# A fourth stream for the attention head, six shared q/k places and an in-place bias in a three-block decoder kernel

## The chip, the cores and the metric

One Trainium2 chip, one core. The metric is device time in microseconds (us) for one execution over the whole batch; it is the median of several runs. Engines: TensorE (PE, with its weight loads PEld), VectorE (DVE), ScalarE (ACT), GpSimd (POOL), SyncE (SP, which here only issues DMAs).

## The reference, cut to what matters

32 sequences of 256 tokens by 512 features pass one post-norm decoder layer of three blocks, each followed by a residual and a layernorm:

```
x = layernorm(x + attention(x, Wqkv, Wout))        # 16 heads of 32, rotary, causal, window 256
x = layernorm(x + mlstm(q=x, k=ctx, v=ctx))        # 4 heads of 128, gates, log-decay, RMS norm
x = layernorm(x + routed_attention(x))             # 4 of 16 heads of 64 picked per sequence,
                                                   # q/k/v with bias, softmax, @ Wo + bo
```

The heads of the third block are picked by a softmax over the token mean of `x @ Wr + br`, so their weights are fetched from HBM by an index that is known only on the chip.

## The kernel before, in words

**Stages and streams.** For each sequence b there are three stages: `stage_a` (first block), `stage_b` (second) and `stage_c` (third). Every engine has a generator for each stage, which does one small step (a group of transposes, one projection, one copy) and yields. Three streams, a, b and c, run over all 32 sequences; `in_turns` merges them by lists, one per engine: a letter says which stream's next step the engine issues. `FILL` starts the pipeline, `ORDER` is repeated `STEADY = NB - 4` = 28 times, one turn for each sequence, and `DRAIN` ends it. In a turn the engines work on stage a of sequence b+1, stage b of b and stage c of b-1. Nothing else sets the order: each engine works its list strictly in order, and semaphores hold it where something isn't ready.

**PSUM.** Four banks `ps_s` hold attention scores, four others are a ring `ps_g`; `BANKS` says which bank of the ring each step uses, and `plan()` derives what must have emptied it (`freed`).

**Stage a.** x is transposed (2 steps), split by ACT (L1033) and DVE (L1288) into a high and a low part `x_t`, and projected with three products per operand pair (L672, `mm3`). For each of four quads of heads (`rotary(u)`) DVE shuffles (L1298) and multiplies by the cosine (L1301), POOL multiplies by the sine (L1655), DVE adds (L1305). `values(t)` gives v. Then per quad: scores, maxes (DVE L1312), exponentials (ACT L1025), transposes of the probabilities (`turn`, copied by ACT L1076 and DVE L1341), product (`att`), scaling (L1358), split (L1103, L1362), and the output projection, the residual (DVE L1368), statistics, `rstd` (POOL L1643, L1645) and x1 (DVE L1381, two instructions). The attended values are written over x_t (`att_t = x_t`), so x of the next sequence can't be split before the output projection of this one is done.

**Stage b.** Transposes of ctx and x1 (copied by ACT L1121), the products for the gates (copied by ACT L1127), gate (DVE L1403), |f| (L1406), exp and ln on ACT, log f (L1410), its running sum on PE (`cum`), a scan, decays, the products c and h, the RMS norm and layernorm, x2 (DVE L1485).

**Stage c.** Transposes of x2, router (`logit`, DVE L1500 to L1524; its index is ready after L1514), the fetch of the picked weights by SP (L648, into `p_all`, `pt_all` and `y_out`), their split (ACT L1188, DVE L1534), q, k, v, scores, softmax, transposes (`fturn`), product (`fatt`, split by ACT L1025 and DVE L1575), output projection (`wo`). POOL adds the bias bo to x2 beforehand (L1707, two instructions), into a tensor of its own, `x2_bo`; DVE adds the projection (L1610); after the layernorm ACT writes `y_out` and stores it (L1256).

**Order around the change, before.** In a steady turn TensorE's list reads, from the end of the output projection of b (b+1, b-1 written as +1, -1):

```
out0 out1 | x2T0-1 xT0+1 ctxT0 xT1+1 ctxT1 x1T0 x2T1-1 x1T1 | qk0+1 gate_t logit-1 gate v0+1 cum SC0+1 a_row
v1+1 m_col decay0 qk1+1 decay1 c0 c1 c2 c3 g-1 SC1+1 h00 h01 h10 h11 ... qk2+1 qk3+1 fturn0-1 ... fturn1-1 att0+1 ...
turn4..7 fturn2-1 att1 fturn3-1 SC3 fatt1-1 turn8..11 wo0-1 att2 wo1-1 turn12..15 att3 out0 out1
```

(`xT`, `x1T`, `x2T`, `ctxT` are transposes, `SC` scores, `v0` is two half steps.)

Of the kernel before, what the change touches and what calls it, by code (L numbers as in the profile page):

```python
# [12 lines left out]
P = 128  # L13
# [48 lines left out]
    "sync": (
        "aaaaaaaaaaaaaaaaaaaaaaaaaaaaaaaaaaaaabaaaaaaaaaaaaaaaaaaaaabaaaaaaaaaaabaaaaaaaaaaaaaaaaaaaaaaaaaaaaaaaaaabaaa"
        "aaaaaaaaaaaaaaaaabaaaaaaaaabaaabaaaaaaaabaabaabaaaabaaaaaaaabaaaabbbaaaabaabaabbbaaaabaabaabbbababaabbaabbaaaa"
        "abaaabaaaacbabbabbbaabbabbbabbbaabbbbaaaaaaaabaabaaaaaabababaaaaaaaaacabaaaaaaaccaabcaaacaaaaabaaaaccaaaccaacb"
        "aaccacaabcaaabaaaaacacaacacacabcacaaabaacaabaccacbcbacaaacababcabacacaaaaaaabbaccccbaaabaaabaabaaccababacacaaa"
        "bacaccbcabbabaaabbbaccbacbcccaabccabaabaaaacaacbccaaaaacacbacbbbcbbbaabc"
# [19 lines left out]
    "gpsimd": (
        "abacbaaababccabaacaabcbbbbaccbabbcccacaabbabbabbabababbcbabcbbbaccbacbabacabccaaabbccbbbbacbccccbaaabbcabbaabc"
        "baaabacccacaaaaaacacccaaacaaaaaaaacaaacaacaacaaacaccaccaccacaaaacaaabaaaaccaacaaaaacaacaaacaaabaaaaaaaacaacaac"
        "aaacabca"  # L90
    ),
    "sync": (
        "acaacaaaccbccbcaabaabbccabaaccbaaabccbbbbbabcacacccccaaaaabababaacbaacacaaabacaaaaaaabcbaaaaacaacabbaacaaaaaaa"
        "aaaabacbabaabbcaacabacbaacaaccabcaccbaabaaaccaacaaacbbbaaaabbaaacaccaccbcacaabaacaababaccaaaccbcbcbbacaccabbaa"
        "aaacbbca"
# [5 lines left out]
        "babcabbcababcbacbababcbbaaabcbbabaababaacacaababbbbbabcbbbcbbcaabcbbacabbbcccaabbbcababbcacccccaaacaccaacaccab"  # L101
        "caaaaccaccacacaaccacacacaacaaaccaacacaaccaccaacbaaaaabcabacaaacaaaaaaacacaaaaaccaaacaaaaaabaaacaaaaabcaaababbc"
        "abaacbabaaabbbbcbbcbccbbbbcbbbbbbbbbbbcbbbccbbbbcbbbcbcccbacbcbccbcccbcccccccccccaccccccbcccccccbcccccbccccccc"
        "cccccccccccccccbccccccccccccccccccccbccccbccccbcccccccccccbcaccccccccc"
    ),
    "scalar": (
        "cbcaababacbabbabbbacacabbcabcbbcabbbababbaaaabcaababcabaaabbcccbbcbacbccbcabbcbabbbbcbacbcbabbabccaccaaacccbaa"
        "cccaaccacaabaaacbacaacacacaaccaaccacaacaacacccacaaaaacacaacaacaacaaaaacaaaaaaacbaaaaaaaaacaaaacaaaabaaaabacaab"
        "abaccbbbcbbabcbaaabbbbbbcbcbbcbcbbbabbabbcbbbbcbbbbccbcbcbccbcccbbbccbcbbccccccccccbccccccccccccccccccccccccbc"
        "ccccaccbcccccccbcccccccccccccccccccbcccccccccccccbcccccccccccccccccccc"  # L110
    ),
    "vector": (
        "babbabcaabbbccabbcaaabbabacabcbcbcbbbcaaabaaaaabbbbaabbbaabbabbbccbcbbbabcbbabbabacabbacccabcaabccacbcccbbcaca"
        "cacaaaacaabcccccacccacaacacaacaccaaccacacaaacaacaacaacaaaaccbbaacaaabcaaabaaaacaaaaaacacacacaaabacababaaaaabab"
        "baaaaabaaacaaccaaaabaaccbcbcbbcbbbbbbcbcbbbcbbbbbbbcbbbcbccbccbcccccccccbbbcccccbcbbbccccccbcccccccccbcccccbcc"
        "ccbcccccbccccccccccccccccccccccccccccccccccccccccccccccccccccccccccccc"
    ),
    "gpsimd": (
        "babcbaabacaccbcbabbbcbabcacbabbbbbbbabbabcaaacbaaaaabaaabcacabbbbbabcabacbacabcbbaaacaacbabcbcabccccabbababbab"
        "bccccacacaaccaaaaccaaacacabaacaaaaaccaaaaaaacaaaacaacaacacabaaaaaaaaacbacccacaaacaaccaaccacbcacaccaacaaaaabaac"  # L120
        "ccabcabbabbaacbacbabbcbabcbbbabbbccbcbccbcbbbbccacccbbbbccbccbcbcbcbbbbccccccbccbbccbbccbcbcccccbccbccccccccbc"
        "ccbcccccccccccccccccccccccccccccccccbccccccccccccccccccccccccccccccccc"
    ),
    "sync": (
        "bcaacabbbaabcaaabaaccaababaaaaaacaaaaaabacbcacaacacbbaaaacbcaabacccbacacaacacabaabaaacacaaacbaaaaccaacaacaccca"
        "bbbaaabbcaaccacbbabccbcaaacbacbccaabaccaccbbcabaacbaaaaaabaabacacbbacbccacaaaaabcabbccccabbccbbacacaacbaacabbc"
        "abbbaacabaaaaacacbaccbccbcbccbcccbcccbcccccbbbbbcccbbbbcbccbcbccbbcccccbcccbbbcccbcbbccccccccbcccccbccbbcbcccb"
        "ccbbbcccbcccbbccccccccccccbccccccccccbcccccccbccccccbccccbcccbccccbccc"
    ),
}  # L130

BANKS = {
# [4 lines left out]
}  # L137

RING = 4
STEADY = NB - 4  # L140
# [53 lines left out]
def build(nc, x, ctx, wqkv, wout, igk, igb, fgk, fgb, rms, wq, bq, wk, bk, wv, bv, wr, br, wo, bo, out):  # L194
# [3 lines left out]

    def halves(name, shape):
        return [sb(f"{name}_{part}", shape, F32R) for part in ("hi", "lo")]  # L200

    def part(pair, *at):
        return [h[at] for h in pair]

# [1599 lines left out]
```

## Time and profile before

| | before |
|---|---|
| median of 3 runs | 2482.59 us (2482.21 to 2490.61) |
| the profiled execution | 2486.7 us, span 2485.0 us |
| busy: PE, DVE, ACT, POOL | 2239.6, 1880.7, 1427.3, 723.9 us |
| mean granted TensorE clock | 0.975 |

The span runs from the first to the last instruction; busy time of an engine is the union of its instructions. A matmul's end is modelled, so a busy PE is not PE at its peak, and short stalls are partly hidden by the tail of the matmul before them. The numbers of L... lines are those of the kernel's file.

### The profile page before, as it was taken

How to read it: one execution, taken by the hardware profiler on the slowest of the kernel's cores; microseconds unless marked ns; L12 is line 12 of the kernel's file. 1: busy time of each engine (PE TensorE's matmuls, PEld its weight loads, DVE VectorE, ACT ScalarE, POOL GpSimd, SP SyncE). 2: the span in 40 equal slices, each digit the busy share in tenths (PEclk: the TensorE clock that was granted, in tenths of full speed). 3: DMA queues.
4: the chain of work that ended last, by engine and by line, in shares of the span. 5: the costliest groups of instructions: out<-in, count | busy, mean ns of one | idle time of the engine just before them, and what ended most of it. 6: DMA issues, size and time to landing. Idle time of an engine off the chain costs nothing.

```text
span 2485.0 us, 55639 instructions
## 1 busy us (share of the span) xinstructions
PE 2239.6 (90%) x20672; PEld 1870.6 (75%) x20672; DVE 1880.7 (76%) x4586; ACT 1427.3 (57%) x4586; POOL 723.9 (29%) x1069
## 2 busy tenths in 40 slices
PE   5888999999999999999999999999999999999864
PEld 4677777877777887778787777878777788877753
DVE  4567788777788877788877787887778788777753
ACT  4445665556566556566655656665665665565632
POOL 2112233222223322323332322332322233222321
PEclk9989999999999999999999999999999999999976
DMA  4010111121011112011121101122211112210111
GB/s 118 18 44 22 49 35 52 52 52 42 29 44 44 52 52 52 27 44 39 48 52 52 44 27 49 38 52 52 52 40 30 44 44 52 52 52 10 43 26 43
DMA packets 267472, 109.94 MB, mean 44 GB/s; under 512 B 215234, under 2 KB 248258, under 8 KB 267202
## 3 DMA queue, kind: packets, MB, share of 16 engines
q1 hardware_dynamic: 258498, 89.61, 14.6%
q10 hardware_dynamic: 8704, 16.78, 1.8%
q8 instruction: 164, 2.69, 0.5%
q14 instruction: 106, 0.87, 0.1%
HBM read 89.57 MB, written 16.78 MB: 43 GB/s over the span
## 4 chain that ended last, share of the span: by engine, by line
PE 44%; DVE 24%; ACT 14%; POOL 5%; issue 5%; SPq 4%; DMA 3%; POOLq 0%; DVEq 0%
PE ps_g L672 32%; PE ps_g L680 10%; ACT p_a L1025 4%; SPq L648 3%; PE ps_s L672 2%; DVE neg_max L1312 2%; DMA y_out<-in_L_ffn_Wv 2%; DVE x_tok L1368 2%; POOL h_ssq L1688 2%; POOL qk_rot L1655 2%; DVE qk L1305 2%; DVE qk_rot L1298 1%; ACT p_all L1025 1%; DVE ctx_t L1473 1%; POOL p_all L1743 1%
## 5 line engine op out<-in xcount | busy, mean ns | idle before, releaser
L1025 ACT ACTIVATE p_a<-ps_s,neg_max 128x128 f32<-128x128 f32 (+1 forms) x1024 | 416.9, 442 | 59.8 <-DVE neg_max L1312 59.7
L672 PE MATMUL ps_g<-x_t_hi,wqkv_hi 128*128 128x256 f32 x1024 | 295.9, 289 | 13.4 <-DVE x_t_lo L1288 13.1
L672 PE MATMUL ps_g<-x_t_lo,wqkv_hi 128*128 128x256 f32 x1024 | 288.6, 282 | 0.0
L672 PE MATMUL ps_g<-x_t_hi,wqkv_lo 128*128 128x256 f32 x1024 | 288.2, 281 | 0.0
L1312 DVE TENSOR_REDUCE neg_max<-ps_s 128x2 f32<-128x256 f32 (+1 forms) x512 | 256.0, 541 | 4.4 <-PE ps_s L672 3.6
L1743 POOL TENSOR_SCALAR p_all<-p_all,f_rec,g_bc 128x256 f32<-128x256 f32 x256 | 144.9, 576 | 359.2 <-DVE f_rec L1561 359.2
L680 PE MATMUL ps_g<-const,p_a 128*128 128x128 f32 x1536 | 225.8, 282 | 15.5 <-ACT p_t L1076 9.2
L1655 POOL TENSOR_TENSOR qk_rot<-qk_rot,const 128x512 f32<-128x512 f32 x128 | 163.8, 1280 | 246.8 <-DVE qk_rot L1298 246.4
L1025 ACT ACTIVATION_READ_ACCUMULATOR p_a<-ps_s,neg_max 128x1 f32 x1024 | 233.8, 228 | 0.0
L680 PEld LDWEIGHTS ps_g<-const,p_a 128*128 128x128 f32 x1536 | 171.7, 143 | 58.8 <-ACT p_t L1076 29.1
L672 PEld LDWEIGHTS ps_g<-x_t_hi,wqkv_hi 128*128 128x128 f32 x1024 | 196.7, 192 | 15.2 <-issue 13.5
L672 PEld LDWEIGHTS ps_g<-x_t_lo,wqkv_hi 128*128 128x128 f32 x1024 | 197.3, 193 | 0.1
L672 PEld LDWEIGHTS ps_g<-x_t_hi,wqkv_lo 128*128 128x128 f32 x1024 | 196.2, 192 | 0.0
L1025 ACT ACTIVATE p_all<-ps_g,f_bias,g_bc 128x256 f32<-128x256 f32 x256 | 142.3, 560 | 68.4 <-DVE f_bias L1556 62.3
L672 PE MATMUL ps_g<-x_t_hi,w_sel_hi 128*128 128x256 f32 x512 | 151.7, 296 | 8.7 <-DVE w_sel_lo L1534 7.5
L1358 DVE TENSOR_TENSOR att_s<-ps_g,r_bc 128x256 f32<-128x256 f32 x128 | 54.3, 424 | 134.2 <-ACT r_bc L1098 131.9
L672 PE MATMUL ps_g<-x_t_hi,w_sel_lo 128*128 128x256 f32 x512 | 143.8, 281 | 0.0
L672 PE MATMUL ps_g<-x_t_lo,w_sel_hi 128*128 128x256 f32 x512 | 143.7, 281 | 0.0
L1195 ACT COPY v_f<-ps_g 128x512 f32<-128x512 f32 x32 | 18.8, 586 | 209.1 <-PE ps_g L672 209.1
L1341 DVE COPY p_t<-ps_g 128x384 f32<-128x384 f32 x256 | 136.0, 541 | 3.7 <-PE ps_g L680 3.6
L1076 ACT COPY p_t<-ps_g 128x384 f32<-128x384 f32 x256 | 119.3, 480 | 23.0 <-PE ps_g L680 20.7
L672 PE MATMUL ps_s<-qk 32*128 32x256 f32 (+1 forms) x2048 | 121.2, 351 | 7.6 <-DVE qk L1305 3.5
(203 smaller groups left out, 6377.0 us busy)
## 6 DMA issues: line engine op xcount, KB each, us to landing
x_tok<-in_x SPq DMA_DIRECT2D x32, 512.0 KB, 3.6
ctx<-in_ctx SPq DMA_DIRECT2D x64, 256.0 KB, 3.4
p_all<-in_L_ffn_Wq SPq DMA_DIRECT2D x128, 128.0 KB, 2.6
pt_all<-in_L_ffn_Wk SPq DMA_DIRECT2D x128, 128.0 KB, 3.0
y_out<-in_L_ffn_Wv SPq DMA_DIRECT2D x128, 128.0 KB, 3.1
out<-y_out ACTq DMA_DIRECT2D x32, 512.0 KB, 2.8
x<-in_L_attn_Wqkv SPq DMA_DIRECT2D x2, 512.0 KB, 9.6
p_all<-in_L_attn_Wqkv SPq DMA_DIRECT2D x1, 512.0 KB, 6.5
```

Source lines behind the costliest of these rows:

```text
L648: engine.dma_start(w_raw[j][:, :, k, :], col((wq, wk, wv)[j])[:, :, bass.ds(picks[k], DF)]).then_inc(w_loaded[j].sem, 16)
L672: return nc.tensor.matmul(o, l, r, start=first, stop=last)
L680: return nc.tensor.transpose(o, i, ident)
L1025: return nc.scalar.activation(o, i, f, **kw)
L1076: nc.scalar.copy(p_t[:, 2 * p % 4, :], bank[("turn", 2 * p), b][:, 0:CAUSAL]).then_inc(act_emptied.sem)
L1305: v.tensor_tensor(qk[:, 2 * u:2 * u + 2, :], qk[:, 2 * u:2 * u + 2, :], qk_rot, ALU.add).then_inc(roped.sem)
L1312: m = v.tensor_reduce(neg_max[i][:, :, t], ps_s[:, 2 * i:2 * i + 2, t * P:t * P + P * (t + 1)], AX.X, ALU.max, negate=True)
L1341: v.tensor_copy(p_t[:, (2 * p + 1) % 4, :], bank[("turn", 2 * p + 1), b][:, 0:CAUSAL]).then_inc(dve_emptied.sem)
L1358: v.tensor_tensor(att_s, bank[("att", u), b][:, 0:T], r_bc, ALU.mult).then_inc(dve_emptied.sem)
L1368: v.tensor_tensor(y_a[b % 2][:, t, :], bank[("out", t), b], x_tok[b % 2][:, t, :], ALU.add).then_inc(dve_emptied.sem)
L1655: g.tensor_tensor(qk_rot, qk_rot, c["sin"].unsqueeze(1).to_broadcast([P, 2, T]), ALU.mult).then_inc(sin_scaled.sem)
L1743: n = g.tensor_scalar(p_f[k % 2][:, t, :], p_f[k % 2][:, t, :], f_rec[:, k, t:t + 1], g_bc[:, k:k + 1], ALU.mult, ALU.mult)
```

## The change

The head of stage a (transposes of x, all four `rotary`, both `values`) becomes a stream of its own, h. The lists have four letters and are all new, so are 12 of the entries of `BANKS`; `STEADY` is `NB - 5`, and `FILL` and `DRAIN` cover one sequence more between them. Core of the rest:

```diff
-STEADY = NB - 4
+STEADY = NB - 5
+SLOTS = 6
+    def slot(b, u):
+        return 2 * ((QUADS * b + u) % SLOTS)
+    def att_t(b, u, cols=slice(None)):
+        return [att_qk[:, slot(b, u) + at, cols] for at in range(2)]
-    qk = sb("qk", [P, 2 * QUADS, T])
+    qk, att_qk = twice("qk", "att_qk", [P, 2 * SLOTS, T])      # one memory, f32 and f32r
-    att_t = x_t
-    q_f = sb("q_f", [P, 2, T])
-    k_f = sb("k_f", [P, 2, T])
+    qk_f, att_f = twice("qk_f", "att_f", [P, 2, 2, T])
-    att_f = [h[:, 0:2, :] for h in x2_t]
-    x2_bo = sb("x2_bo", [P, TT, D])
-    y_c = x2_bo
+    x2_bo = x2
+    y_c = y_out
# ACT, split of x
-                    act.wait_ge(*full[("out", TT - 1), b - 1])
+                    act.wait_ge(*full[("qk", QUADS - 1), b - 1])
# ACT, copy of v
+                    act.wait_ge(*full[("att", QUADS - 1), b - 1])
# DVE, rotary: cosine product into slot(b, u)
-                    dve.wait_ge(*scored(b - 1))
+                before = QUADS * b + u - SLOTS
+                if before >= 0:
+                    dve.wait_ge(*full[("out", TT - 1), before // QUADS])
# ACT, split of x2
-                    act.wait_ge(*full[("wo", TT - 1), b - 1])
+                    act.wait_ge(*full[("vf",), b - 1])
# DVE, x2
-                dve.wait_ge(*full[("x2", TT - 1), b - 1])
-                dve.wait_ge(*with_bo(b - 1))
+                dve.wait_ge(*empty[("wo", TT - 1), b - 1])
# DVE, q and k of the third block
+                    dve.wait_ge(*full[("wo", TT - 1), b - 1])
# POOL, bias
-            pool.wait_ge(*x2_made(b))
-            if b:
-                pool.wait_ge(*y_made(b - 1))
-            for t in range(TT):
+            for t in range(TT):
+                pool.wait_ge(*full[("x2", t), b])
                 g.tensor_tensor(x2_bo[:, t, :], x2[:, t, :], bo_s, ALU.add).then_inc(with_bo.sem)
```

Every instruction keeps its operation and its shape. What the new lists give in a steady turn, written as above:

```
out0 out1 | xT0+1 ctxT0 ctxT1 xT1+1 x2T0-1 x2T1-1 x1T0 x1T1 | qk0+1 logit-1 gate_t v0a+1 gate v0b+1 cum SC0+1 a_row
v1+1 m_col decay0 qk1+1 decay1 c0 c1 c2 g-1 c3 h00 SC1+1 h01 h10 h11 ... qk2+1 qk3+1 fturn0-1 ... fturn1-1 att0+1 ...
turn4..7 fturn2-1 att1 fturn3-1 SC3 turn8 turn9 fatt1-1 turn10 turn11 wo0-1 att2 wo1-1 turn12..15 att3 out0 out1
```

- DVE, before: `out0 out1 stats x1 x-split0+1 x-split1+1 x2-split-1 rotary0+1 gate |f| log f`, the last addition of rotary0, then the router. After: `out0 out1 stats x-split0+1 x1 x-split1+1 x2-split-1`, the first router step, all of rotary0, then gate, |f| and log f, and the router's index ahead of the copy of `cum`. x2 (L1485) moves from ahead of att1's scaling to ahead of att3's, the last two router-block maxima and `fturn2`'s copy move by one or two places.
- POOL, before: `rstd_a`, sine of rotary0, bias, .... After: `rstd_a`, bias, sine of rotary0, ....
- ACT: all three weight splits (L1188) stand ahead of the copies of h00 and h01, where before the third stood behind them; v1's copy stands ahead of the decays.
- SP: same order in a steady turn.
- Banks of note: ctxT and out1 share bank 2, x2T1 takes over bank 3 from xT0, c2 moves from bank 1 (qk1's) to 3, h11 from 0 to 1 (h01's), gate and `gate_t` stay in 0.

## Rows read from the trace of the kernel before

**Rows 1.** The page: busy time by engine

```profile
PE 2239.6 (90%) x20672; PEld 1870.6 (75%) x20672; DVE 1880.7 (76%) x4586; ACT 1427.3 (57%) x4586; POOL 723.9 (29%) x1069
```

**Rows 2.** Stores of out, in two stretches: ns min/median/max, first and last start

```profile
L1256 ACTq DMA_DIRECT2D out<-y_out x29: 378/378/422, 226.9 to 2275.9; - x29
...
L1256 ACTq DMA_DIRECT2D out<-y_out x4: 378/378/379, 520.9 to 739.5; - x4
```

**Rows 3.** Busy time by stretch: PE, PEld, DVE, ACT, POOL, clock, DMA share, GB/s

```profile
0.00:62.00 62.00, 34.38 (x319) 29.80 (x320) 27.30 (x53) 26.74 (x72) 13.74 (x17) 0.95 0.43 118
...
2298.00:2485.00 187.00, 127.08 (x901) 101.31 (x899) 99.31 (x241) 72.89 (x212) 43.99 (x72) 0.78 0.15 37
```

**Rows 4.** Waits of PE, three turns (1545 to 1764.3): us in total, times, longest

```profile
PE ps_g L680 <- ACT ctx_t L1121: 4.9, 6, 1.4
PE ps_g L680 <- DVE p_t L1341: 3.0, 3, 1.0
PE ps_g L680 <- DVE qk L1301: 1.3, 3, 0.6
...
PE ps_g L672 <- DVE m_parts L1428: 0.8, 3, 0.3
```

**Rows 5.** Timeline from 1616 to 1632: start, us, engine, line, what [idle before <- releaser]

```profile
1618.66 1.38 DVE L1368 TENSOR_TENSOR x_tok<-ps_g,x_tok 128x512 f32<-128x512 f32 x2 [1.20 <-PE ps_g L672]
...
1620.19 0.63 PE L680 MATMUL ps_g<-const,x_tok 128*128 128x128 f32 x4 [0.44 <-DVE x_tok L1368]
...
1620.65 0.60 PE L680 MATMUL ps_g<-const,ctx 128*128 128x128 f32 x4
...
1621.29 0.59 ACT L1121 COPY ctx_t<-ps_g 128x512 f32<-128x512 f32 x1 [2.85 <-PE ps_g L680]
...
1622.59 1.00 DVE L1381 TENSOR_SCALAR x<-x_tok,ln_mv_a,ln_rstd_a 128x512 f32<-128x512 f32 x2 [1.15 <-POOL ln_rstd_a L1645]
...
1623.98 1.53 PE L680 MATMUL ps_g<-const,x 128*128 128x128 f32 x12 [1.39 <-ACT ctx_t L1121]
```

**Rows 6.** Timeline from 1629 to 1636, gate to cum, and the router's index

```profile
1629.78 0.61 PE L672 MATMUL ps_g<-const,decay 128*128 128x8 f32 x4
1630.37 2.55 POOL L1707 TENSOR_TENSOR x_bo<-x,bo_s 128x512 f32<-128x512 f32 x2
1630.63 1.06 DVE L1406 SCALAR_TENSOR_TENSOR g_abs<-gate 128x8 f32<-128x8 f32 x1
1632.20 0.74 DVE L1410 SCALAR_TENSOR_TENSOR log_f<-gate,g_ln 128x8 f32<-128x8 f32 x1 [0.51 <-ACT g_ln L1025]
1633.09 0.52 PE L672 MATMUL ps_g<-log_f,const 128*128 128x8 f32 x4
...
1635.19 0.16 DVE L1514 FIND_INDEX8 r_idx<-r_dtop,r_dist 1x8 uint32<-1x16 f32 x1
```

**Rows 7.** Timeline from 162 to 166, the same steps in the fill

```profile
163.21 0.51 PE L672 MATMUL ps_g<-const,decay 128*128 128x8 f32 x4
...
163.97 0.17 DVE L1406 SCALAR_TENSOR_TENSOR g_abs<-gate 128x8 f32<-128x8 f32 x1
...
164.87 0.61 PE L672 MATMUL ps_g<-log_f,const 128*128 128x8 f32 x4 [0.16 <-DVE log_f L1410]
```

**Rows 8.** Timeline from 2279.5 to 2283, bias and x1

```profile
2279.95 2.67 POOL L1707 TENSOR_TENSOR x_bo<-x,bo_s 128x512 f32<-128x512 f32 x2
2280.01 2.89 DVE L1381 TENSOR_SCALAR x<-x_tok,ln_mv_a,ln_rstd_a 128x512 f32<-128x512 f32 x2 [1.14 <-POOL ln_rstd_a L1645]
```

**Rows 9.** L1188 from 300 to 2200, x26 for each weight: who released them

```profile
  DMA pt_all<-in_L_ffn_Wk: 8.3, 14
  DMA y_out<-in_L_ffn_Wv: 6.2, 11
```

**Rows 10.** Timeline of PE from 1667 to 1683: fatt1, wo0

```profile
1677.12 1.08 PE L672 MATMUL ps_g<-pt_all,v_f 128*64 128x256 f32 x8
...
1679.56 0.47 PE L672 MATMUL ps_g<-wo_hi,x_t_hi 128*128 128x512 f32 x1
```

More of the change, by code:

```diff
@@ L96 @@
+        "abbhcaba"
     ),
@@ L200, in halves, with twice @@
         return [sb(f"{name}_{part}", shape, F32R) for part in ("hi", "lo")]
+    def twice(name, again, shape):
+        with nc.sbuf_tensor(name, shape, F32) as one:
+            pass
+        return one.ap(), nc.alloc_sbuf_tensor(again, shape, F32R).ap()
+    def slot(b, u):
+        return 2 * ((QUADS * b + u) % SLOTS)
+    def att_t(b, u, cols=slice(None)):
+        return [att_qk[:, slot(b, u) + at, cols] for at in range(2)]
     def part(pair, *at):
@@ L273, in build @@
     b_v = sb("b_v", [P, KF // 2])
-    q_f = sb("q_f", [P, 2, T])
-    k_f = sb("k_f", [P, 2, T])
+    qk_f, att_f = twice("qk_f", "att_f", [P, 2, 2, T])
+    q_f, k_f, att_f = qk_f[:, 0], qk_f[:, 1], [att_f[:, at] for at in range(2)]
     v_f = sb("v_f", [P, TT, KF * DF])
@@ L381, in stage_a @@
             yield from values(0)
+            yield from values(1)
+            for u in range(1, QUADS):
+                yield from rotary(u)
+        def stage_a(b):
             for _ in range(5):
                 yield
-            yield from values(1)
-            yield from rotary(1)
             for u in range(QUADS):
@@ L582, in stream @@
                 yield from stages[n](b)
-        live = {n: stream(n) for n in "abc"}
+        live = {n: stream(n) for n in "habc"}
         for n in FILL[engine] + ORDER[engine] * STEADY + DRAIN[engine]:
@@ L624, in stage_a @@
                 load_x(b + 1)
-            for _ in range(QUADS * 4 + TT * 3 + 5 + QUADS * 20 + TT * 2 + 1):
+            for _ in range(QUADS * 4 + TT * 3):
+                yield
+        def stage_a(b):
+            for _ in range(5 + QUADS * 20 + TT * 2 + 1):
                 yield
@@ L721, in values, with stage_a @@
                 yield
+            yield from rotary(0)
+            yield from values(0)
+            yield from values(1)
+            for u in range(1, QUADS):
+                yield from rotary(u)
+        def stage_a(b):
             def projected(t, first, last):
@@ L725, in projected @@
                 for k in range(first, last):
-                    done = mm3(bank[("out", t), b], part(att_t, slice(None), k, slice(t * P, (t + 1) * P)), part(wout_s, slice(None), k), k == 0, k == KT - 1)
+                    done = mm3(bank[("out", t), b], att_t(b, k, slice(t * P, (t + 1) * P)), part(wout_s, slice(None), k), k == 0, k == KT - 1)
                 return done
@@ L744, in scores @@
                 done.then_inc(scored.sem)
-            yield from rotary(0)
-            yield from values(0)
             scores(0)
@@ L750, in stage_a @@
                 yield
-            yield from values(1)
-            yield from rotary(1)
             for u in range(QUADS):
@@ L1039, in values, with stage_a @@
                 act.wait_ge(*full[("v", t), b])
+                if b:
+                    act.wait_ge(*full[("att", QUADS - 1), b - 1])
                 nc.scalar.copy(v_a[:, t, :], bank[("v", t), b]).then_inc(act_emptied.sem)
                 yield
+            for _ in range(4):
+                yield
+            yield from values(0)
+            yield from values(1)
+            for _ in range(3 * 4):
+                yield
+        def stage_a(b):
             def exps(p):
@@ L1055, in exps @@
                 e.then_inc(exped.sem)
-            for _ in range(4):
-                yield
-            yield from values(0)
             for _ in range(3):
@@ L1063, in stage_a @@
                 exps(p)
-                yield
-            yield from values(1)
-            for _ in range(4):
                 yield
@@ L1090, in stage_a @@
                     yield
-                if u == 0:
-                    for _ in range(2 * 4):
-                        yield
                 yield
@@ L1101, in stage_a @@
                 act.wait_ge(*empty[("att", u), b])
-                act.wait_ge(*full[("qk", QUADS - 1), b])
-                nc.scalar.copy(att_t[0][:, u], att_s).then_inc(att_hi.sem)
+                nc.scalar.copy(att_t(b, u)[0], att_s).then_inc(att_hi.sem)
                 yield
@@ L1304, in rotary, with stage_a @@
                 dve.wait_ge(*empty[("qk", u), b])
-                v.tensor_tensor(qk[:, 2 * u:2 * u + 2, :], qk[:, 2 * u:2 * u + 2, :], qk_rot, ALU.add).then_inc(roped.sem)
+                v.tensor_tensor(qk[:, slot(b, u):slot(b, u) + 2, :], qk[:, slot(b, u):slot(b, u) + 2, :], qk_rot, ALU.add).then_inc(roped.sem)
                 yield
+            yield from rotary(0)
+            for _ in range(3 + 3):
+                yield
+            for u in range(1, QUADS):
+                yield from rotary(u)
+        def stage_a(b):
             def maxes(p):
@@ L1313, in maxes @@
                 m.then_inc(maxed.sem)
-            yield from rotary(0)
-            for _ in range(4):
-                yield
+            yield
             maxes(0)
@@ L1320, in stage_a @@
             maxes(1)
-            for _ in range(3 + 3):
+            for _ in range(3):
                 yield
-            yield from rotary(1)
             for u in range(QUADS):
@@ L1658, in stage_a @@
             yield from rotary(0)
-            for _ in range(3 + 5 + 3):
+            for _ in range(3 + 3):
                 yield
-            yield from rotary(1)
-            for _ in range(15):
-                yield
-            yield from rotary(2)
-            yield from rotary(3)
-            for _ in range(5 + (QUADS - 1) * 20 + 2 * TT):
+            for u in range(1, QUADS):
+                yield from rotary(u)
+        def stage_a(b):
+            for _ in range(5 + QUADS * 20 + 2 * TT):
                 yield
```

177 lines of the change are left out of this document (91 added, 86 removed), and 6 rows, old and new, of the table BANKS.

## The prediction, made before the changed kernel ran

> **What bounds the kernel now.** I read the page first: TensorE is busy 90% of the span, DVE 76%, ACT 57% [rows 1]. So TensorE comes close to being the bound, and what is left to win is the time in which it waits. Next the stores of the output, one for each sequence: 29 of them from 226.9 to 2275.9, that is 28 turns of 73.2 us [rows 2]. The two ends are told by the stretches: in the first 62 us PE is busy 34.4 us, in the last 187 us 127.1 us, there with a mean granted clock of 0.78 of full speed [rows 3]. So the time is about 227 us of fill, 28 turns of 73.2, and 206 us of drain. A turn is the place to look at: 0.45 us in each makes 12.4 us, which is 0.5% and about what a measurement of this kernel can tell from no change.
>
> Inside a turn PE's waits name few places. In three turns: 4.9 us for ACT's copies of ctx (L1121), 3.0 us for DVE's copy of probabilities (L1341), 1.3 us for a cosine product that frees a bank (L1301), 0.8 us for the parts that the decays need (L1428) [rows 4]. The first is the border between two sequences. There DVE adds the residuals from 1618.66, PE gets a bank back at 1620.19, DVE starts x1 at 1622.59, after POOL's rstd, and PE can transpose x1 only at 1623.98 [rows 5]. That chain, 4.8 us from the end of the output projection (1619.15, 0.49 after the first add began), is covered by five blocks of transposes of 0.46 us (from 1620.19 to 1620.65 [rows 5]), and the rest is idle.
>
> **The change part by part.** *The fourth stream.* It would pay if q, k and v of the next sequence moved into the waits of this one. The order that the lists give doesn't do that: the projections of q and k stand where they stood, 2 and 3 still ahead of att0, 0 still behind the border. No instruction is added or dropped, so PE's work per turn stays, and only the small permutations count. The new waits (the split of x on the last q/k product, the cosine on the output projection two sequences back, v on att3, x2 on the last add of wo, q_f on wo) each name something that already stands ahead in the order of the queue or a quarter of a turn back; behind each of them DVE and ACT have the whole rest of their queue, but they are passed before they are reached. I cost them at 0. Should one bind, it is late by the time between the two steps, and the waits of that size that exist are the 1 us kind of [rows 4]. The store moves 0.7 us later, because DVE's shift now follows att3's split; ACT was idle 2.85 us there [rows 5], so 0. SP's queue keeps its order.
>
> *The border.* xT0 now goes at once (bank 3 is free), ctxT0 takes bank 2 from out1 at 1620.19, as xT0 did. ACT's copy follows 0.64 later (1620.65 to 1621.29 [rows 5]), takes 0.59, so ctxT1 goes at 1621.47, then xT1, x2T0 (at 1622.37) and x2T1. Six blocks instead of five stand ahead of x1T0, one less behind it. But x1T0 still goes when x1 is made, at 1623.98, and q/k 0 behind it needs bank 2 back from ACT's copy of x1T0, 0.64 + 0.59 + 0.05 = 1.28 later, at 1625.3. Before, the three blocks from 1623.98 ended at the same time. Gain 0. DVE's split of xT0, put ahead of x1, ends at about 1622.6 (ACT's two copies end at 1621.9, the split takes 0.68), just when rstd comes: 0.
>
> *The bias and the gates.* Before, bias ran on POOL from 1630.37 for 2.55 us, and DVE's |f| took 1.06 and log f 0.74 us inside it [rows 6]; in the fill, where they were clear of it, |f| took 0.17, and from gate to `cum` were 1.66 us instead of 3.31 [rows 7, 6]. Now bias goes ahead of rotary0's sine, some 6 us before the gates. The lists use that up: between gate and `cum` stands one half step of v instead of two. After: gate at 1631.0, that is 1629.78 and a half step of v, 1.4 us (3.31 less gate's own 0.46, halved), less the 0.2 us for which gate waited for ACT's copy of gate_t, which v0a now covers. From there `cum` needs the 1.66 us of [rows 7] and 0.2 for rotary0's add, which stands ahead of gate on DVE: 1632.9, where it was at 1633.09. So scores 0 come 0.2 us earlier. The router's index, ready at 1635.35 [rows 6] behind `cum`'s copy, follows log f directly in the new list: 1632.7 and five small operations of 0.17 each, 1633.55, 1.8 us earlier. With max0 no longer held up by it, the wait for the decay's parts (0.8/3 [rows 4]) goes. Sum: 0.5 us by `decay0`.
>
> *Behind it.* c2 in another bank saves some part of the L1301 wait, at most 1.3/3 us a turn and at least nothing, since fturn1 waits for the same line; I take 0.2. Against that h11 waits for ACT's copy of h01, which now stands behind all three weight splits: between nothing and about 1 us (a split has 1024 elements a partition, twice the 0.59 us copy of [rows 5]); I take 0.3, as the third split's landing is the only thing that can be late. What remains of the gain at att1 is set by DVE, which works without a gap from the c products up to the copy of the probabilities that att1 waits for (L1341, 1.0 us [rows 4]), so it is what DVE's queue has gained: 0.5 us. Then fatt1, two turns later, ends at 1678.9 instead of 1678.15, and its split, of ACT and DVE, comes 0.45 us later than wo0 wants it (1679.56); before, fatt1 and four turns filled 2.44 us up to wo0 without a wait [rows 10]. att2 follows wo0 directly, so all of this is on the path: minus 0.45. A turn thus wins 0.05 us: 27 x 0.05 = 1.4 us.
>
> *The weights.* ACT waited for Wk in 14 of 26 turns (8.3 us) and for Wv in 11 (6.2 us) [rows 9]; turns without such a wait take 72.9 us (218.6 for three [rows 2]), the mean is 73.2, which makes 28 x 0.3 = some 9 us over the run. The fetch now starts 1.8 us earlier, the split of Wk wants it only 1.1 us earlier, that of Wv 2.6 us earlier. So Wk's share goes, 9 x 8.3/14.5 = 5.2 us, and Wv's stays. Fill and drain have nearly the same order: 0, between -5 and +5 us, some 6% of the 28 and 60 us for which PE is idle there [rows 3].
>
> *Sum.* 2486.7 (the profiled execution's own time; its span is 2485.0) - 1.4 - 5.2 = 2480.1. The median is 4.1 below that execution, so **2476 us**.
>
> **The rivals.** *Slower: bias meets x1.* x2T0 is issued at 1622.37, so bias may start on POOL at about 1623.05; the second of the two L1381 starts at 1622.59 + 0.46 = 1623.05 (two take 1.00, the unstretched one 0.54). Where the two met in the drain, x1 took 2.89 us instead of 1.00 [rows 8, 5], so they exclude each other, as with |f| in [rows 6]. If POOL asks first, x1 ends at about 1624.7 instead of 1623.6, x1T0 waits that 1.1 us, and everything behind it: 27 x 1.1 = 30 us on 2476, 2506 us. It decides within 0.1 us: x2T0 earlier, or x1 later than I have them, and it happens in every turn. For it speaks that an added split stands ahead of x1; against it that DVE's second instruction is queued before POOL's is released.
> The Trainium skill (SBUF — State Buffer, "Who interferes with whom") says that DVE and GpSimd share a port pair as an exclusive lock for whole instructions, when DVE is in a 2-port mode or reads two SBUF inputs. The rows agree: the L1381 pair is stretched, as is |f|. By that rule alone the first to ask wins, and it doesn't say who that is here.
>
> *Faster: fatt1 costs nothing.* If ACT's split of fatt1 and DVE's follow fast enough (my 0.45 us rests on three latencies of 0.1), or DVE's queue wins more up to att1 than I see (the last maxima, frec), a turn wins 0.5 to 0.7 us: with the weights 2482.6 - 27 x 0.6 - 5.2 = 2461 us. For it speaks that the front part's gain is on PE already at the decays.
>
> *Nothing but noise of the fetch.* Wv, wanted 2.6 us earlier with 1.8 us given, now holds ACT with h00 and h01 behind it; if it is 1 us in 11 turns of 26, passed on through h11's bank: 27 x 11/26 x 1 us = 11 us lost in place of 5.2 won, 2492 us. Against it: on average Wv was late by 6.2/11 = 0.6 us only [rows 9].
>
> **How the numbers follow.** The forecast 0.36; bias on x1 0.27; the cheap fatt1 0.29; the fetch 0.08. The forecast case spans 2468 to 2484, the faster one 2450 to 2470, the collision 2495 to 2515. The range from 2454 to 2507 leaves out about a tenth at each end. Faster by over 0.5% (below 2470.2): 0.29 and a fifth of the forecast's, 0.36. Slower by over 0.5% (above 2495): 0.29. Within: 0.35.
>
> **What would show it.** Step by step in the profile after: PE's blocks at the border end with x1T0 4.8 us after the output projection; |f| at 0.17 and log f at 0.17 us; L1381 at 0.54 (stretched to 1.5: the collision); a wait of PE on L1575's tile ahead of wo0, about 0.4 us a turn; fewer waits of L1188 for Wk; turns of 72.7 to 72.9 us between stores. Wrong would be: turns below 72.3, x1T0 earlier than 4.6 us after the projection (then I missed what frees it), or q and k steps of the next sequence inside PE's waits after all.

## The result, and the profile after

The changed kernel takes **2511.82 us** (median of 4 runs, 2508.82 to 2516.12), beside 2483.93 us for the kernel before on the same chip: a ratio of 1.0114 (95% interval 1.0101 to 1.0127), 1.1% slower. The forecast was 2476 us, and the result lies 5 us above the upper end of the range, next to the rival "bias meets x1" (2506 us). The profiled execution of the changed kernel is the one of 2516.12 us, its span is 2514.4 us.

The page and the stores of `out` (ns min/median/max, first and last start), which answer to [rows 1, 2]:

```profile
PE 2258.1 (90%) x20672; PEld 1868.0 (74%) x20672; DVE 1871.8 (74%) x4586; ACT 1428.0 (57%) x4586; POOL 728.5 (29%) x1069
...
L1285 ACTq DMA_DIRECT2D out<-y_out x29: 378/378/422, 234.6 to 2306.0; - x29
L1285 ACTq DMA_DIRECT2D out<-y_out x28: 378/378/379, 316.0 to 2306.0; - x28
```

The same row for the 28 stores of the kernel before, in the same manner:

```profile
L1256 ACTq DMA_DIRECT2D out<-y_out x28: 378/378/379, 301.1 to 2275.9; - x28
```

These rows divide the loss. The first store is 7.7 us later than in [rows 2], the second 14.9 us (316.0 less 301.1), the 29th 30.1 us, and the last (2511.2, before 2481.8) 29.4 us. So the fill with its first turn costs 14.9 us, and 27 turns cost 15.2 us: a turn takes (2306.0 - 316.0) / 27 = 73.70 us, before 73.14. The drain costs nothing.

PE's waits in three turns (1570 to 1791: us in total, times, longest), beside [rows 4]:

```profile
PE ps_g L709 <- DVE x L1412: 3.7, 3, 1.2
PE ps_g L709 <- DVE p_t L1375: 2.7, 3, 0.9
PE ps_g L709 <- ACT ctx_t L1150: 2.0, 3, 0.7
PE ps_g L709 <- DVE x_tok L1399: 1.3, 3, 0.4
PE ps_g L701 <- DVE att_f L1607: 0.9, 3, 0.3
PE ps_g L709 <- DVE qk L1331: 0.8, 3, 0.4
```

The first row is new. The line that makes x1 (L1412, before L1381) was no releaser in [rows 4], and now costs 1.2 us in every turn, while the waits for `ctx_t` fell from 4.9 to 2.0 us, those for the cosine from 1.3 to 0.8, and the one for `m_parts` is gone. It is so throughout: of the 48 instructions of L1412 from 400 to 2200 every second one is stretched (mean 1063 ns, in e1 below 543). The border between two sequences, timeline from 1643 to 1651, beside [rows 5]:

```profile
1644.08 0.60 PE L709 MATMUL ps_g<-const,x_tok 128*128 128x128 f32 x4
...
1645.12 0.62 PE L709 MATMUL ps_g<-const,ctx 128*128 128x128 f32 x4 [0.44 <-DVE x_tok L1399]
...
1646.42 0.66 PE L709 MATMUL ps_g<-const,ctx 128*128 128x128 f32 x4 [0.68 <-ACT ctx_t L1150]
...
1647.35 1.04 PE L709 MATMUL ps_g<-const,x 128*128 128x128 f32 x8
1647.54 2.04 DVE L1412 TENSOR_SCALAR x<-x_tok,ln_mv_a,ln_rstd_a 128x512 f32<-128x512 f32 x2
...
1648.03 2.68 POOL L1736 TENSOR_TENSOR x<-x,bo_s 128x512 f32<-128x512 f32 x2 [0.53 <-PE ps_g L709]
...
1649.63 1.25 PE L709 MATMUL ps_g<-const,x 128*128 128x128 f32 x8 [1.25 <-DVE x L1412]
...
1650.96 0.39 PE L701 MATMUL ps_g<-x_t_hi,wqkv_hi 128*128 128x256 f32 x1
```

Read it from the fifth row: DVE starts the pair of instructions that make x1 at 1647.54. POOL starts the bias 0.49 us later, as soon as PE has transposed x2, and the pair takes 2.04 us instead of the 1.00 of [rows 5]. PE has nothing left but x1's transposes and stands still for 1.25 us. From gate to `cum`, beside [rows 6, 7]:

```profile
1656.75 0.51 PE L701 MATMUL ps_g<-const,decay 128*128 128x8 f32 x4
...
1657.54 0.17 DVE L1437 SCALAR_TENSOR_TENSOR g_abs<-gate 128x8 f32<-128x8 f32 x1
...
1658.22 0.17 DVE L1441 SCALAR_TENSOR_TENSOR log_f<-gate,g_ln 128x8 f32<-128x8 f32 x1 [0.51 <-ACT g_ln L1054]
...
1658.59 0.50 PE L701 MATMUL ps_g<-log_f,const 128*128 128x8 f32 x4
```

What the bias did to |f| and log f (1.06 and 0.74 us) it now does to x1. ACT's weight splits from 300 to 2200 (26 for each weight), beside [rows 9], and fatt1 and wo0, beside [rows 10]:

```profile
  DMA y_out<-in_L_ffn_Wv: 20.6, 26
  DMA pt_all<-in_L_ffn_Wk: 2.0, 4
```

```profile
1702.89 1.08 PE L701 MATMUL ps_g<-pt_all,v_f 128*64 128x256 f32 x8
1705.07 0.50 PE L701 MATMUL ps_g<-wo_hi,att_f 128*128 128x512 f32 x1 [0.29 <-DVE att_f L1607]
```

The waits for Wk went from 8.3 to 2.0 us, but those for Wv rose from 6.2 us in 11 turns to 20.6 us in all 26.

### The profile page after: what moved, and what is told of

Read it like the earlier page. It is cut to its first block, busy times and chain, and to the rows that moved or that the text cites. A ratio compares the mean times of both kernels' runs of the same rounds, so it can differ in the third digit from the quotient of the medians.

```text
span 2514.4 us, 55679 instructions
## 1 busy us (share of the span) xinstructions
PE 2258.1 (90%) x20672; PEld 1868.0 (74%) x20672; DVE 1871.8 (74%) x4586; ACT 1428.0 (57%) x4586; POOL 728.5 (29%) x1069
## 4 chain that ended last, share of the span: by engine, by line
PE 39%; DVE 24%; ACT 13%; POOL 9%; issue 7%; SPq 6%; DMA 3%; POOLq 0%; DVEq 0%
PE ps_g L701 30%; PE ps_g L709 8%; SPq L677 4%; ACT p_a L1054 4%; POOL qk_rot L1687 3%; DMA y_out<-in_L_ffn_Wv 2%; PE ps_s L701 2%; POOL h_ssq L1719 2%; POOL x L1736 2%; DVE x_tok L1399 2%; DVE ctx_t L1504 2%; DVE neg_max L1349 2%; DVE f_max L1585 2%; POOL p_all L1772 2%; DVE qk L1335 2%
## 5 line engine op out<-in xcount | busy, mean ns | idle before, releaser
L701 PE MATMUL ps_g<-x_t_hi,wqkv_hi 128*128 128x256 f32 x1024 | 296.4, 289 | 18.7 <-DVE x_t_lo L1317 14.6
L1349 DVE TENSOR_REDUCE neg_max<-ps_s 128x2 f32<-128x256 f32 (+1 forms) x512 | 257.2, 544 | 23.6 <-PE ps_s L701 22.6
L701 PE MATMUL ps_g<-wout_hi,att_qk 128*128 128x512 f32 x512 | 178.2, 409 | 0.1
L1389 DVE TENSOR_TENSOR att_s<-ps_g,r_bc 128x256 f32<-128x256 f32 x128 | 54.3, 424 | 136.9 <-ACT r_bc L1128 134.4
```

The lines of the kernel that those rows point to most:

```text
L701: return nc.tensor.matmul(o, l, r, start=first, stop=last)
L1349: m = v.tensor_reduce(neg_max[i][:, :, t], ps_s[:, 2 * i:2 * i + 2, t * P:t * P + P * (t + 1)], AX.X, ALU.max, negate=True)
L1389: v.tensor_tensor(att_s, bank[("att", u), b][:, 0:T], r_bc, ALU.mult).then_inc(dve_emptied.sem)
```

## The experiments

All runs in one table. "To 29th" is the mean of the 27 turns from the second store to the 29th, "rest" is from there to the last store. Ratios are to the kernel before on the same chip, with their 95% interval; its median was 2483.4 to 2485.1 us in the four sessions, so medians of different sessions compare to some 2 us. The store columns rest on one trace for each kernel, and executions of the kernel after lie up to 7 us apart, so a difference of 0.1 us a turn is not told from none.

| kernel | median us | ratio | 1st, 2nd store | to 29th | rest |
|---|---|---|---|---|---|
| before | 2483.93 | 1 | 226.9, 301.1 | 73.14 | 205.9 |
| after | 2511.82 | 1.0114 [1.0101, 1.0127] | 234.6, 316.0 | 73.70 | 205.2 |
| e1 bias behind x1 | 2484.99 | 1.0000 [0.9991, 1.0009] | 231.2, 312.7 | 72.80 | 205.3 |
| e2 four places | 2513.87 | 1.0116 [1.0101, 1.0132] | 233.5, 314.9 | 73.74 | 203.8 |
| e3 fill from ORDER | 2490.06 | 1.0024 [1.0015, 1.0033] | 216.1, 289.6 | 73.84 | 203.4 |
| e5 e1 and e3 | 2459.36 | 0.9898 [0.9883, 0.9913] | 215.7, 288.2 | 72.72 | 202.6 |
| g1 before, bias early | 2574.40 | 1.0359 [1.0345, 1.0373] | 228.5, 304.5 | 76.20 | 203.9 |
| g2 before, bias early but behind x1 | 2474.20 | 0.9955 [0.9942, 0.9969] | 228.4, 302.1 | 72.96 | 200.9 |
| f1 e1, fatt1 back | 2483.89 | 0.9997 [0.9988, 1.0006] | 232.9, 312.8 | 72.72 | 204.2 |
| f2 e1, third split back | 2468.73 | 0.9933 [0.9920, 0.9947] | 231.7, 313.1 | 72.13 | 203.3 |
| h1 SP's fill alone | 2509.19 | 1.0110 [1.0094, 1.0125] | 232.6, 312.4 | 73.62 | 203.3 |
| h2 all fills but SP's | 2488.24 | 1.0018 [1.0009, 1.0028] | 216.5, 289.6 | 73.66 | 204.8 |
| f3 e5 and f2 | 2442.26 | 0.9836 [0.9823, 0.9850] | 214.8, 286.8 | 72.05 | 204.5 |
| f4 f3, turn 7's bank | 2441.28 | 0.9832 [0.9819, 0.9846] | 216.1, 288.1 | 72.07 | 203.6 |

**e1, the bias waits for x1.** One line in POOL's stage c of the changed kernel; the lists stay.

```diff
             for _ in range(2 * TT):
                 yield
+            pool.wait_ge(*x1_made(min(b + 1, NB - 1)))
             for t in range(TT):
                 pool.wait_ge(*full[("x2", t), b])
```

> The bias of x2 on POOL waits for the x1 of the next sequence, so that the two can't meet on the port; nothing else is changed. My theory (the collision stretches x1 from 1.0 to 2.0 us in every turn and all of it lies on PE's path): L1412 falls to 0.54 us each, x1T0 no longer waits 1.2 us, a turn between stores falls from 73.70 to 72.7 us (the 73.14 of before less the 0.45 that the other parts of the change were to win), and the whole from 2512 to about 2485 us. Rival (the collision is hidden, and the 0.56 us per turn come from the later stalls behind fatt1 and turn 7): L1412 falls too, but the turn stays within 0.2 us of 73.7, the whole 2506 to 2513. Second rival (the collision moves, the later bias now meets |f| and log f as it did before): turn 73.1 to 73.4, whole 2495 to 2505.

The timeline of the border with the wait:

```profile
1624.54 0.60 PE L709 MATMUL ps_g<-const,x_tok 128*128 128x128 f32 x4
...
1628.00 1.00 DVE L1412 TENSOR_SCALAR x<-x_tok,ln_mv_a,ln_rstd_a 128x512 f32<-128x512 f32 x2
...
1629.06 1.25 PE L709 MATMUL ps_g<-const,x 128*128 128x128 f32 x8 [0.21 <-DVE x L1412]
1629.08 2.53 POOL L1737 TENSOR_TENSOR x<-x,bo_s 128x512 f32<-128x512 f32 x2 [1.11 <-DVE x L1412]
...
1630.39 0.38 PE L701 MATMUL ps_g<-x_t_hi,wqkv_hi 128*128 128x256 f32 x1
```

x1 takes 1.00 us again, PE waits 0.21 us for it, and the kernel is 26.8 us faster (2511.82 to 2484.99): in the traces 0.91 us in each of the 27 turns, which makes 24.5, and 3.3 in the fill. The theory expected about 2485. The bias starts 4.54 us behind xT0 instead of 3.95, and it meets nothing there that counts.

**g1 and g2, the kernel before with the bias moved.** In POOL's list of the kernel before, the bias of the sequence two back goes ahead of rotary 0's sine product; g2 has all three lines, g1 lacks the wait.

```diff
+                if u == 0 and b >= 2:
+                    pool.wait_ge(*x1_made(b - 1))
+                    bias(b - 2)
                 pool.wait_ge(*shuffled(b, u + 1))
```

> The kernel before with one thing moved: POOL adds x2's bias ahead of rotary 0's sine product instead of behind it, with no wait for x1. It then follows rstd directly on POOL, just as DVE starts x1. My theory (the two exclude each other, and x1 is on PE's path at the border): x1 takes up to 2.9 us instead of 1.0 as in [rows 8], |f| and log f fall to 0.17; a turn goes from 73.14 to 73.14 + 1.9 - 0.5 = 74.5 us, the whole from 2485 to about 2522 us. Rival (the border has slack in this kernel): the turn falls by up to 0.5 us, the whole 2471 to 2485 us.

> The same, but the bias waits for x1. No collision with x1, and the gates' small operations are clear of the bias too. My theory (the gates' chain by decay0 wins 0.3 to 0.5 us and it stays on PE's path): turn 72.6 to 72.85, the whole from 2485 to 2471 to 2477 us; so all that the change wins per turn is this one move. Rival (what is won at the decays is lost again ahead of att1, where DVE's queue decides): turn within 0.1 of 73.14, the whole 2482 to 2488 us.

g1's border, timeline:

```profile
1603.38 2.67 POOL L1652 TENSOR_TENSOR x_bo<-x,bo_s 128x512 f32<-128x512 f32 x2
1603.44 2.89 DVE L1381 TENSOR_SCALAR x<-x_tok,ln_mv_a,ln_rstd_a 128x512 f32<-128x512 f32 x2 [1.14 <-POOL ln_rstd_a L1645]
...
1606.38 1.99 PE L680 MATMUL ps_g<-const,x 128*128 128x128 f32 x10 [2.95 <-DVE x L1381]
```

POOL is first by 0.06 us, and x1 takes 2.89 us, as in [rows 8]. But the turn grew by 3.06 us (73.14 to 76.20), not by the 1.4 that was expected, and the whole takes 2574 us, 52 more than expected. The rest is the clock. Busy time by stretch (PE, PEld, DVE, ACT, POOL, granted clock, DMA share, GB/s) right behind the wait:

```profile
1606.00:1607.00 1.00, 0.62 (x5) 0.44 (x5) 1.00 (x3) 0.00 (x0) 0.04 (x1) 1.00 0.00 0
1607.00:1608.00 1.00, 1.00 (x7) 0.97 (x7) 1.00 (x2) 0.59 (x1) 0.00 (x0) 0.59 0.47 129
1608.00:1609.00 1.00, 1.00 (x6) 1.00 (x5) 0.72 (x2) 0.16 (x1) 0.00 (x0) 0.50 0.83 322
1609.00:1610.00 1.00, 1.00 (x7) 1.00 (x6) 0.05 (x1) 0.92 (x2) 0.00 (x0) 0.50 0.20 74
1610.00:1611.00 1.00, 1.00 (x8) 1.00 (x7) 1.00 (x2) 0.00 (x0) 0.00 (x0) 0.70 0.00 0
1611.00:1612.00 1.00, 1.00 (x11) 1.00 (x10) 0.24 (x1) 0.00 (x0) 0.00 (x0) 1.00 0.02 8
```

After 2.95 us in which PE did nothing the granted clock is 0.50 (1.2 of 2.4 GHz) for over two microseconds, and the second to fifth row, in which PE is busy throughout, lose 0.41 + 0.50 + 0.50 + 0.30 = 1.7 us of full speed. In the next two turns it is 1.7 and 1.4 us, and the mean granted clock of the run is 0.956, before 0.975. PE's wait ahead of x1T0 grew by 1.56 us (2.95, in [rows 5] 1.39), less than the 1.89 by which x1 is stretched, since x1 was not what PE waited for there. So 1.56 us of wait and 1.4 to 1.7 us of clock, less the 0.2 us that g2 wins, make 2.8 to 3.1 us, and the turn grew by 3.06. In the kernel after the wait is 1.25 us and the clock in that stretch stays at 1.00, as it does in the kernel before behind 1.39 us, so there the collision costs its own length and no more.

g2 shows the other side: with the bias early and clear of x1 the kernel before wins 9.5 us (0.9955), 27 x 0.18 = 4.9 us of it in the turns and 5.0 us in the drain (205.9 to 200.9), where [rows 8] had the same collision. The gain per turn lies below the 0.3 to 0.5 expected, between both theories: the wait for `m_parts` (6.0 us from 400 to 2200) is gone, and the waits for the cosine rose from 14.6 to 16.7 us.

**e2, four places.** `SLOTS = 6` becomes 4.

> Four q/k places in place of six. Theory (the lists never use the two more: the projections of q and k stand where they stood, so the wait on the output projection of the sequence whose place is overwritten is passed long before): 2512 us, within 3. Rival (the places do let a rotary step run ahead of the last output projection): the cosine product waits for the output projection of the sequence just before, 1 us or more in each turn, 2540 us or more.

2513.87 us, the turn 73.74: no change. The two more places, the change's headline, are not used by its lists.

**e3, the fill's order.** The lists of the first turns are no longer the given ones, but the steady list of each engine, without the steps whose sequence doesn't exist yet.

```diff
+def filled_by(engine, turns):
+    steps = ORDER[engine] * turns
+    left = {s: steps.count(s) - FILL[engine].count(s) for s in set(steps)}
...
+FILL = {engine: filled_by(engine, 5) for engine in FILL}
```

> Only the order of the first turns is changed: each engine's FILL list is made from the steady ORDER list (its leading steps left out where the work doesn't exist yet), the steady turns and the drain stay. Theory F (the fill's own list interleaves the second turn badly and costs the 14.9 us up to the second store): the second store comes 5 to 10 us earlier, the gap from first to second store falls from 81.4 to about 74, whole 2500 to 2506. Rival G (the new fourth stream itself, by its places, banks and waits, makes the first turns slow, whatever the order): gap stays at 80 or more, whole 2510 to 2520. In both the turns from the second store on stay at 73.7 us.

The first store is 18.5 us earlier and the second 26.4 us; the whole is 21.8 us faster, more than the 6 to 12 expected, though the 27 turns give back 3.6 us of the 26.4. Busy time by stretch, columns as above, before (first row), after and then e3:

```profile
62.00:100.00 38.00, 29.90 (x217) 23.59 (x216) 16.73 (x40) 14.94 (x52) 2.25 (x3) 0.86 0.05 15
```

```profile
62.00:100.00 38.00, 28.69 (x200) 22.09 (x200) 13.37 (x34) 9.75 (x32) 2.23 (x3) 0.87 0.04 15
100.00:140.00 40.00, 29.91 (x304) 24.23 (x305) 27.05 (x65) 24.52 (x95) 9.87 (x12) 0.87 0.05 14
140.00:180.00 40.00, 33.33 (x246) 27.35 (x245) 20.07 (x56) 16.96 (x51) 8.21 (x14) 0.92 0.23 54
```

```profile
62.00:100.00 38.00, 33.30 (x271) 26.53 (x272) 20.69 (x52) 18.52 (x63) 5.09 (x8) 1.00 0.05 15
100.00:140.00 40.00, 28.56 (x295) 23.26 (x288) 24.72 (x58) 19.72 (x73) 7.48 (x7) 0.91 0.05 15
140.00:180.00 40.00, 37.02 (x335) 32.69 (x334) 31.12 (x78) 18.83 (x53) 13.85 (x19) 1.00 0.27 67
```

With the fill as given, PE does 200 matmuls from 62 to 100 at a clock of 0.87, with the steady order 271 at 1.00: PE waits more, and what it does between the waits goes at a lower clock. In the given list scores 0 of the next sequence stand ahead of the gates of this one, in the steady list behind them; no run tried that pair alone. And the second store is 11.5 us earlier than in the kernel before, whose own fill does 217 matmuls at 0.86 in that stretch: the edit takes out more than the change put in. Whether the kernel before would gain as much by a fill made from its own `ORDER`, no run shows.

**h1 and h2, whose list it is.** e3's edit for SP alone, and for the other four.

> The changed kernel with only SP's part of FILL made from ORDER; the other four engines keep FILL as it is. SP's list says when the loads of ctx, x and the picked weights are issued in the first turns. Theory F1 (the fetches come late in the fill): this alone wins most of the 22 us that the whole edit won, 2492 to 2500 us. Theory F2, mine (the loss is in the order of the work of the computing engines, PE waits for DVE's x1 and copies in the second turn): 2509 to 2514 us, no change.

> The mirror of it: PE, ACT, DVE and POOL take the FILL made from ORDER, SP keeps its own. Theory F2 (order of the computing engines): 2489 to 2495 us, the whole gain of 22 us, first store at about 216 us and the gap to the second near 73.5. Theory F1: 2505 us or more, with waits for loads at the first weight splits.

2509.19 and 2488.24 us: the order of the four computing engines brings the gain, that of the loads does not. SP's list alone moves the second store by 3.6 us. Which of the four lists it is, no run shows.

**e5, both edits.**

> Both edits together: bias behind x1, and FILL made from ORDER. If the two costs are separate and both lie in what each edit touches, their gains add: 2512 less 27 less 6 to 12, that is 2473 to 2479 us. If the fill's loss is the collision as well (its first turns meet it too), this comes out the same as the bias edit alone, about 2485 us.

2459.36 us. The single gains are 26.8 and 21.8 us, together they win 52.5: they add, and 4 us more. The turn keeps e1's gain, the fill e3's.

**f1, fatt1 back.** On e1, the order of three queues:

```diff
-PE   att1 fturn3 SC3 turn8 turn9 fatt1
+PE   att1 fturn3 SC3 fatt1 turn8 turn9
-DVE  att1's scaling, copy of fturn2
+DVE  copy of fturn2, att1's scaling
-ACT  split of att1, copy of fturn3
+ACT  copy of fturn3, split of att1
```

> The changed kernel with the bias behind x1 (2485 us, turns of 72.80), and on top of it fatt1 back directly behind scores 3 on PE, with the two copies that it needs ahead of att1's split on DVE and ACT as in the kernel before. My theory (the later fatt1 makes wo0 wait for its split, 0.3 to 0.45 us a turn): that wait goes, turn 72.35 to 72.5, whole 2473 to 2477 us. Rival (the wait only moves to turns 8 and 9 or to att2, which now come later behind fatt1): 2483 to 2487 us.

2483.89 us beside 2484.99: the rival. Waits of PE from 400 to 2200, e1 and then f1:

```profile
PE ps_g L709 <- DVE p_t L1375: 22.5, 25, 1.0
PE ps_g L709 <- ACT ctx_t L1150: 16.2, 24, 0.7
PE ps_g L701 <- ACT h_raw L1187: 10.9, 19, 1.4
...
PE ps_g L701 <- DVE att_f L1607: 7.3, 25, 0.3
```

```profile
PE ps_g L709 <- DVE p_t L1375: 30.7, 50, 1.0
```

The wait for `att_f` (7.3 us) is gone, and 8.2 us of waits for `p_t`, in 25 more places, stand in its place.

**f2, the third split back.** On e1, ACT's list:

```diff
-ACT  split q, split k, split v, em, copy h00, copy h01, copy h10
+ACT  split q, split k, em, copy h00, copy h01, split v, copy h10
```

> The changed kernel with the bias behind x1 (2485 us), and on top of it ACT's third weight split back behind the copies of h00 and h01. My theory (h11 waits for a bank that ACT empties late, because ACT waits for the last weight to land, 28 us over the run, before it copies h): PE's waits for h_raw fall from 12 us to near 0, turn down by 0.3 to 0.45 us, whole 2473 to 2477 us. Rival (the split itself is wanted by the first q_f product, which now comes late in its place): 2483 to 2490 us.

2468.73 us, 16.3 us faster than e1 where 8 to 12 were expected, with turns of 72.13 us. PE's waits on `h_raw` (10.9 us above) are gone, and the splits hardly wait for a load any more, from 300 to 2200:

```profile
ACT w_sel_hi L1217 <- DMA pt_all<-in_L_ffn_Wk: 2.0, 4, 1.0
ACT w_sel_hi L1217 <- DMA y_out<-in_L_ffn_Wv: 0.8, 2, 0.6
```

In e1 ACT waited 21.9 us for Wv in the same stretch and 3.1 for Wk. So it stood 0.8 us a turn waiting for Wv with the copies of h00 and h01 behind it. The turn gains 0.67 us, more than PE's 0.44 of waits on `h_raw`; which of ACT's later steps brings the rest no run separates.

**f3 and f4, all three, and one bank.** f3 puts e1, e3 and f2 together; f4 also moves turn 7.

```diff
-    "turn": "0232102001211023",
+    "turn": "0232102101211023",
```

> All three edits on the changed kernel: bias behind x1, FILL made from ORDER, third weight split behind h00 and h01. If the costs are separate, as I hold, their gains add: 2459.4 us of the two, less the 16 us of the split, 2441 to 2446 us, 1.6% under the kernel before, turns of 72.1 us. Rival (the splits' gain and the fill's overlap): 2450 us or more.

> All three edits and one more: turn 7 writes PSUM bank 1 (free since turn 4's copy by ACT) in place of bank 0, for which it waits 0.9 to 1.0 us in each turn until DVE has copied turn 5 (the largest wait that is left). Theory (DVE's queue decides here, its copies, maxima and products follow each other without a gap, so the wait only moves from turn 7 to r_wide and att1 behind it): same as without it within 2 us. Rival (PE's wait on the bank is what delays turn 7's copy on DVE): 10 us faster or more.

f3 takes **2442.26 us, 1.6% under the kernel before** (0.9836) and 2.8% under the kernel after. f4 is the same within 1 us. Waits of PE from 400 to 2200 (lines are 14 higher than in the kernel after, L1389 is the copy of probabilities), f3 and then f4:

```profile
PE ps_g L723 <- DVE p_t L1389: 22.6, 25, 1.0
PE ps_g L723 <- ACT ctx_t L1164: 16.9, 25, 0.7
```

```profile
PE ps_g L723 <- POOL p_all L1787: 18.1, 25, 0.7
PE ps_g L723 <- ACT ctx_t L1164: 16.9, 25, 0.7
```

The largest wait in the list was worth nothing: take away its bank, and PE waits 18.1 us in the next step (fturn2) for POOL and 7.8 us for ACT's copies of probabilities, together more than the 22.6 that went.

## Why the prediction failed

**The race of bias and x1 was worked out rightly and then weighed wrongly.** The prediction had x2T0 issued 3.22 us after the output projection and the bias 0.46 us behind the start of x1; the trace has 3.27 and 0.49. It priced the collision at 1.1 us a turn and 30 us in all; e1 gives 26.8. What failed is the sentence "against it that DVE's second instruction is queued before POOL's is released", for which it took 0.27 as the chance. DVE's pair is two instructions, and POOL, released as the second was due, got in ahead of it, in every turn, not in some. That is read from the durations: one of the two is stretched when POOL starts behind the first, both when it starts ahead. The Trainium skill (SBUF — State Buffer, "Who interferes with whom") says that issue order, and not the kind of operation, decides who is blocked. The lengths of the pair agree: DVE clear of POOL 1.00 us (e1), POOL between the two 2.04 (after), POOL ahead of both 2.89 (g1). No run here shows POOL as the one that is held up.

**Fill and drain at 0, between -5 and +5**: right for the drain (-0.7 us), wrong for the fill. It was costed by "nearly the same order", while `FILL` is a list of its own, and no step of the new one was followed. It lost 14.9 us up to the second store, of which 3.3 are the collision (e1) and the rest the order of the four computing engines (e3, h2). With the collision this is what put the result outside of the range: the range held either, not both, and it cut the collision's own span (2495 to 2515) at 2507.

**The border at 0**: without the collision x1T0 goes 4.52 us after xT0 in e1, before it went 4.83 us after the projection; q/k 0 comes 5.85 instead of 6.13. A gain of 0.28 us a turn was missed. The row of [rows 5] says why: x1T0 waited for ACT's copy of ctxT1, not for x1. The prediction took it as x1's time, and 4.52 lies below the 4.6 that it had named as a sign of this. That q/k 0 then follows 1.28 us behind x1T0 was right (1.33).

**The gates**: gate 7.0 us behind x1T0 and `cum` 1.86 us behind it were forecast; 7.12 and 1.84 were measured, |f| and log f at 0.17. What it is worth on the path, 0.5 us, was too much, as far as g2 tells, which wins 0.18 us a turn with the bias moved in the lists of the kernel before.

**fatt1 at +0.45**: PE's wait on its tile is there (0.29), but f1 shows that it costs 0.08 us a turn. That is no more than noise. The wait stands where another one would, so the step was mis-sized by 0.37, and this much of the rival "cheap fatt1" held, though not the turn that it forecast.

**The weights**: Wk's waits went as forecast (8.3 to 2.0 us). The sum behind them is a little off: 28 x 0.3 is 8.4 us, not 9, and Wk's share of that 4.8, not 5.2. That "Wv's stays" is wrong: 6.2 became 20.6, and with h11 behind it the third split costs 0.67 us a turn (f2), where the prediction had 0.3. The mechanism was the fetch rival's, at 1 us in 11 turns of 26; it is 0.8 us in all 26, because in the new list the split is wanted before Wv lands, in every turn.

**That the places change nothing** was right (e2). That DVE's queue decides around turn 7 fits f4's time; what PE waits for then is POOL, and that POOL in turn follows DVE there is argued, not shown.

Between the forecast for the profiled execution (2480.1) and its 2516.12 lie 36.0 us. The collision makes 24.5 + 3.3 of them and the fill's order 11.6. The other misses, over 27 turns, are +10.0 for the third split, +8.6 for the gates, -10.0 for fatt1 and -7.6 for the border; that they nearly cancel is luck, and 4 us the other way stay open.

Added up for a turn: +0.91 collision, +0.67 third split, +0.08 fatt1, -0.18 gates, -0.28 border; the 0.56 measured leaves -0.64 for the rest. Of that the rows show the waits for the cosine (14.6 to 7.3 us from 400 to 2200, 0.3 a turn) and for ACT's `p_t` (7.9 to none, 0.3); how much of each lies on the path no run separates. And the change is a good one that two orders spoil: its steady lists, freed of the collision and the early split, take 72.13 us a turn, before 73.14.

## What to carry to other kernels

When a step is moved out of one collision, look up what runs on the shared resource at its new place, and if the margin there is less than the step itself, order the two by a wait: one line here was worth 27 us. Cost the fill's list separately from the steady one, since it can lose more than the turns gain: in e1 the new turns win 27 x 0.34 = 9 us, and the fill loses 11.6. And a wait at the head of the list is worth only what the next one behind it leaves: f1 and f4 removed 7 and 22 us of waits, got 8 and 26 us of others and won no more than 1 us each. f2 removed 11 us and won 16; there ACT's own waits for weights went too, from 25.0 to 2.8 us.

## What the runs showed of the hardware

A pair of DVE instructions is no unit towards POOL: in the kernel after a POOL addition that starts 0.49 us after the pair began stretches the second from 0.53 to 1.59 us (L1412, longest 1587 ns, shortest 534), and itself only grows from 2.53 to 2.68 us for its two. With POOL ahead by 0.06 us (g1) the DVE pair takes 2.89 us and POOL's 2.67. In both orders it is DVE that pays nearly everything.

A wait of 2.95 us of TensorE cost more than 2.95 us. In g1 it was followed in the three turns looked at by a stretch at a granted clock of 0.50, worth 1.7 us more in the one shown; waits of 0.44, 0.68 and 1.25 us at one border, in the kernel after, were not, nor were 0.44, 0.24 and 1.39 us in the kernel before.
